# Expert 0's low weight parts move from GpSimd to VectorE, and the combine-weight products move behind the first step's second half

## What is computed

```
logits = einsum(x, gate_w); weights, indices = top_k(softmax(logits), 2), normalised
for i in 0..7:
    h   = silu(x @ w1[i]) * (x @ w3[i])        # 256 -> 1024
    out = out + (h @ w2[i]) * w_of_expert_i     # 1024 -> 256
```

## Time and profile before

| | us |
|---|---|
| median of 3 runs | 495.22 |
| the three runs | 494.84, 495.22, 1086.1 |
| span of the profiled execution (first to last instruction) | 492.8 |
| what lies around the span, by the median | 2.4 |
| own time of the profiled execution | not given beside its span |
| TensorE busy | 422.1 (86% of the span) |
| VectorE busy | 263.6 (53%) |
| ScalarE busy | 192.5 (39%) |
| GpSimd busy | 169.9 (34%) |
| mean granted TensorE clock | 0.926 |

### The profile page before, as it was taken

How to read it: one execution, slowest core, us unless ns; L and a number is a source line. 1 busy time by engine, 2 the same in 40 slices (tenths; PEclk the granted TensorE clock), 3 DMA queues, 4 the chain that set the end, 5 groups by cost and what they waited for, 6 DMA issues and landing times.

```text
span 492.8 us, 10407 instructions
## 1 busy us (share of the span) xinstructions
PE 422.1 (86%) x2557; PEld 365.9 (74%) x2558; DVE 263.6 (53%) x670; ACT 192.5 (39%) x334; POOL 169.9 (34%) x133
## 2 busy tenths in 40 slices
PE   0678984314999999999999999999999999999980
PEld 0556864313888889888888988888898888889870
DVE  7877869997454255433563564355356433653230
ACT  3446443301444246233542643354264334542230
POOL 5455434442023333322242333224233322532321
PEclk9979795555999999999999999999999999999995
DMA  6856885604415421541118118111811211121120
GB/s 196 297 179 206 272 268 157 200 1 139 161 23 160 149 32 32 203 105 23 30 21 287 32 21 283 32 26 21 287 32 21 32 30 23 21 32 32 21 32 11
DMA packets 33076, 50.92 MB, mean 103 GB/s; under 512 B 3335, under 2 KB 25095, under 8 KB 33063
## 3 DMA queue, kind: packets, MB, share of 16 engines
q1 hardware_dynamic: 24983, 38.44, 23.4%
q0 software_dynamic: 8080, 12.33, 12.8%
HBM read 39.36 MB, written 11.40 MB: 103 GB/s over the span
## 4 chain that ended last, share of the span: by engine, by line
PE 73%; DVE 7%; issue 2%; DMA 1%; POOL 1%; ACT 1%; ACTq 0%; POOLq 0%; DVEq 0%
PE bank L1312 64%; PE bank L1335 7%; PE bank L1319 2%; DVE ctx_sb L901 2%; DVE onehot_lo L986 1%; DVE rank L889 1%; DMA dg<-depool_rows,plugi 1%; PE bank L1266 1%; POOL dg L441 1%; DMA xblk<-z_rows,gidx 1%; PE bank L1191 0%; DVE batch L990 0%; POOL out L485 0%; DVE st L823 0%; DVE x_all L820 0%
## 5 line engine op out<-in xcount | busy, mean ns | idle before, releaser
L1312 PE MATMUL bank<-split,xT_hi 128*128 x592 | 166.8, 403 | 1.3 <-DVE xT_lo L1087 1.3
L1096 DVE TENSOR_TENSOR hmul<-gact,bank 128x512 f32<-128x512 f32 x74 | 50.9, 688 | 149.1 <-ACT gact L614 149.1
L485 POOL DMA_INDIRECT out<-yblk,itok x37 | 78.4, 2118 | 149.8 <-ACT yblk L621 138.2
L1312 PEld LDWEIGHTS bank<-split,xT_hi 128*128 128x128 f32 x592 | 106.9, 190 | 22.6 <-issue 1.9
L1312 PE MATMUL bank<-split,hT 128*128 (+1 forms) x888 | 115.4, 286 | 1.4 <-issue 0.8
L1312 PEld LDWEIGHTS bank<-split,hT 128*128 128x128 f32 x888 | 108.5, 191 | 2.1 <-issue 1.2
L614 ACT ACTIVATE gact<-bank 128x512 f32<-128x512 f32 x74 | 44.2, 598 | 158.9 <-PE bank L1312 158.8
L1312 PE MATMUL bank<-split,xT_lo 128*128 x296 | 93.7, 398 | 0.0
L477 POOL DMA_INDIRECT xblk<-z_rows,gidx x40 | 40.1, 1001 | 106.0 <-DVE gidx L1109 100.3
L321 DVE TENSOR_TENSOR split<-raw,split x21 | 48.1, 2293 | 37.6 <-ACT split L315 37.6
L1312 PEld LDWEIGHTS bank<-split,xT_lo 128*128 128x128 f32 x296 | 56.0, 189 | 13.5
(11 more groups left out here) (182 smaller groups left out, 332.4 us busy)
## 6 DMA issues: line engine op xcount, KB each, us to landing
raw<-in_L_ffn_w SPq DMA_DIRECT2D x24, 1024.0 KB, 8.0
ctx_sb<-in_ctx SPq DMA_DIRECT2D x4, 1024.0 KB, 6.4
x_all<-in_x SPq DMA_DIRECT2D x4, 512.0 KB, 8.3
depool_rows<-gact SPq DMA_DIRECT2D x4, 512.0 KB, 3.0
out<-x_all SPq DMA_DIRECT2D x4, 512.0 KB, 5.5
z_rows<-z SPq DMA_DIRECT2D x4, 512.0 KB, 3.9
xblk<-z_rows,gidx POOLq DMA_INDIRECT x40, 2.8
out<-yblk,itok POOLq DMA_INDIRECT x37, 4.7
```

What stands on the lines that cost most here:

```text
L485: pool.indirect_dma_start(out[:, :], bass.IndirectOffsetOnAxis(ap=itok[:, q:q + 1], axis=0), yblk[:, q, :], None, compute_op=ALU.add).then ...
L1096: dve.tensor_tensor(hmul[:, cols], gact[:, cols], p_lin[part][:, :], ALU.mult)\
L1312: mm = pe.matmul(out_, xp, w_, start=start and n == 0, stop=stop and n == 2)
```

## The change

GpSimd no longer makes low parts. VectorE makes those of w1 and w3 in two halves by columns, the first half of both ahead of `xT(0, 0)` and the second half ahead of `weight_rows`, and that of w2 at the end of step 0. TensorE waits for `lo_first` 1 and 2 ahead of the two halves of `up` in step 0; for step 1 it waits, as before, for `lo_ready`, which now rises at the end of VectorE's step 0. The list products of the combine weights stand behind `up(0, 1)` instead of behind `up(0, 0)`.

```
--- before.py
+++ after.py
@@ -458,17 +458,12 @@
                     pow2(k - 2)
 
 
-            split_lo(pool, 0, 0, 0, "lo_first")
-            split_lo(pool, 0, 0, 1, "lo_first")
-
-
             pool.wait_ge(s["hi_step"], 1)
             pool.wait_ge(s["bf16_ready"], 14)
             half = slice(0, B * TPB)
             pool.tensor_tensor(hi_idx[:, half, 1, :], hi_eq[:, half, :],
                                tiles_b[:, half].unsqueeze(2).broadcast_to([P, B * TPB, TABLE]), ALU.mult)\
                 .then_inc(s["tile_step"], 1)
-            split_lo(pool, 0, 0, 2, "lo_first")
 
             def block_rows(i, q):
 
@@ -1115,6 +1110,14 @@
                 dve.tensor_copy(wtok[:, q:q + 1], w_all[:, ds(i, 1)])
                 dve.tensor_copy(itok[:, q:q + 1], idx_all[:, ds(i, 1)]).then_inc(s["meta_ready"], 1)
 
+            def first_up(part):
+
+                cols = slice(part * HALF, (part + 1) * HALF)
+                dve.wait_ge(s["hi_ready"], 2)
+                dve.tensor_tensor(up_lo[:, 0, :, :, cols], raw_up[:, 0, :, :, cols],
+                                  up_hi[:, 0, :, :, cols].bitcast(f32), ALU.subtract)\
+                   .then_inc(s["lo_first"], 1)
+
             def step(i, q, half, word):
                 later = not isinstance(i, int) or i > 0
                 h(i, 0)
@@ -1127,6 +1130,10 @@
                     weights_out()
                 h(i, 1)
                 hT(i, q, 0)
+                if not later:
+                    split_lo(dve, 0, 0, 2, "lo_first")
+                    dve.wait_ge(s["lo_first"], 3)
+                    dve.sem_inc(s["lo_ready"], 3)
 
                 with dve.If(word & F_CHUNK):
                     e = expert(word)
@@ -1141,10 +1148,10 @@
             dve.wait_ge(s["x1_rows"], 16 * B)
             for b in range(B):
                 dve.wait_ge(z_out[b], 16)
-            dve.wait_ge(s["lo_first"], 3)
-            dve.sem_inc(s["lo_ready"], 3)
+            first_up(0)
             xT(0, 0)
             next_index(2, 0, 1)
+            first_up(1)
             weight_rows(0)
             weight_rows(1)
             def drain(i, q):
@@ -1354,16 +1361,21 @@
                 later = not isinstance(i, int) or i > 0
                 slot = word & 1
                 pe.wait_ge(s["xTlo_ready"], i + 1)
-                pe.wait_ge(s["lo_ready"], expert(word) * 3 + 2)
+                if later:
+                    pe.wait_ge(s["lo_ready"], expert(word) * 3 + 2)
+                else:
+                    pe.wait_ge(s["lo_first"], 1)
 
                 up(slot, q, 0)
-                if not later:
-                    lists(p_w, hi_w, (8, 11))
                 if later:
                     hT(i - 1, 1)
                 xT(i + 1, 1 - q, half + q)
 
+                if not later:
+                    pe.wait_ge(s["lo_first"], 2)
                 up(slot, q, 1)
+                if not later:
+                    lists(p_w, hi_w, (8, 11))
                 hT(i, 0)
                 if later:
                     down(i - 1, 1 - q, expert_before(word), (word >> PREV_BIT) & 1)
```

## The result

488.61 us median (488.37 to 489.01, 4 runs) beside 494.84 for the kernel before (493.31, 494.84 and 495.22): a ratio of 0.9888, 95% interval 0.9869 to 0.9907, so it is some 1.1% faster, which is clear of the noise. One further run of the kernel before took 1086.1 us and is left out. The forecast was 491.7 with 488.2 to 495.0, so the time lies in the range, at its lower end. It lies outside the narrower 490.3 to 493.3 that the prediction gave the forecast itself, and 0.3 us from what rival (a) gave. The profiled execution took 488.38 us with a span of 486.7; the one of before has 492.8, a difference of 6.1 us, and what follows accounts for that.

What follows compares the result with a forecast made beforehand. The prediction took the time as when the blocks start plus TensorE's work in the steps; -10.5 + 0.4 + 4.3 - 0.5 + 2.4 + 0.4 = -3.5 us on 495.2 gave 491.7 us, range 488.2 to 495.0.

Steps and rivals of the forecast that it cites:

- rival (a): TensorE's clock holds through the 4.3 us wait and step 0 gets it as before: -6.3, 488.9 us; chance 0.18.
- The gain, -10.5: Router, ahead of the table: three VectorE stalls beside GpSimd's low parts leave, 2.3 + 3.9 + 4.3 = 10.5 us earlier.
- the first stall: VectorE's cast of 8 elements beside GpSimd's first low part: 4.1 us raw, of which 2.3 us come through.
- rival (b): The first stall isn't GpSimd's doing, or something else holds the last batch: -1.2, 494.0 us; chance 0.10.
- Rival (d): TensorE at half clock holds the router's chain, so only the third stall comes through: +2.7, 497.9 us; chance 0.02.
- The first half ahead of step 0, +0.4: VectorE's 2.29 us low part ahead of `xT_lo` exceeds its idle 2.05 us: `up(0, 0)` starts 0.4 us later.
- The wait of step 1, +4.3: Ahead of `up(1, 0)` TensorE stands idle 4.3 us for the low part of w2; bounds 3.8 and 4.8.
- Given back, -0.5: Step 1's own wait for VectorE, 0.44 us visible at 136.29, goes: -0.5 us (0.2 to 1.0).
- The clock, +2.4 and +0.4: TensorE's clock falls after step 1's wait, +2.4 us (0 to 3.4); step 0 must also earn it, +0.4 (0 to 1.2).
- (c): The clock stays low well beyond step 1; through two whole steps it costs 9.5, 498.8 us; chance 0.04.

Runs made afterwards that it cites:

- experiment 5: The changed kernel plus an unread GpSimd instruction, the low part of w1 at its old place: 491.41 us.
- experiment 7: The changed kernel plus an unread GpSimd instruction, the low part of w3 at its old place: 492.41 us.
- experiment 9: The changed kernel plus an unread GpSimd instruction, the low part of w2 at its old place behind GpSimd's list product: 492.97 us.
- experiment 6: The changed kernel plus half of w1's low part (1024 of 2048 columns) on GpSimd at its old place, unread: 489.20 us.
- experiment 2: The changed kernel with the low part of w2 made in VectorE's idle time ahead of `weights_out`, not at the end of step 0: 483.43 us.
- experiment 3: The changed kernel with `lo_ready` raised in two parts, so step 1 starts without w2's low part and only the down product waits for it: 485.04 us.
- experiment 1: The changed kernel with 34 unused transposes of the identity filling TensorE's wait at the end of step 0: 486.38 us.
- the seven executions: The profiled executions with the wait at the end of step 0: one each of the changed kernel, experiment 4, experiment 5, experiment 6, experiment 7, experiment 8 and experiment 9.
- experiment 11: The kernel of experiment 2 with 16, 5 and 5 unused transposes in TensorE's waits between the index lists and step 0: 483.33 us.
- experiment 4: The changed kernel with the combine-weight list products back behind the first half of `up` in step 0: 489.04 us.
- experiment 8: The changed kernel plus a GpSimd memset of 2048 float32 a partition behind its list product, where w2's low part was: 490.08 us.
- experiment 12: The kernel of experiment 2 with the unused transposes of experiment 11 and GpSimd's last list product made by VectorE: 482.83 us.

## Why the prediction was right, term by term

**The gain, -10.5.** Measured 10.8 (10.9 less 0.15), and experiments 5, 7 and 9 give its parts: 2.6, 3.9, 4.3 for 2.3, 3.9, 4.3. The reason for the first number, that TensorE's logits cover the first two us of the first stall, is shown by experiment 6: half an instruction holds VectorE for 2.0 us longer and costs 0.4 in the trace, and the transposes start only 0.1 us later. What the sum left out is that they run 0.3 us shorter behind the logits. The rival (b), that the one-input cast isn't held by GpSimd, fell with experiment 5. Rival (d) fell with the table at 105.12.

**The first half ahead of step 0, +0.4.** Measured +0.1. `xT_lo` started 0.3 us later against the table than before, about as the sum had it, but TensorE's 0.43 us between `xT_lo` and its first matmul became 0.23, so most of the delay was taken up. Why that interval is shorter wasn't tried.

**The wait of step 1, +4.3.** Measured +4.03, and its cause, the low part of w2 at the end of VectorE's queue, is shown by experiments 2 and 3, which each take the gap ahead of step 1 away. Neither `up(0, 1)` nor the list products waited for VectorE, as forecast.

**Given back, -0.5.** Step 1 gave back 1.0 us where the clock is kept (experiment 1, 12.64 us for 13.60), and the same in the changed kernel (0.58 lost in all, of which the clock took 1.56). I had counted little more than the visible 0.44 us at 136.29 and named 1.0 as the bound. The rest is what a break costs the matmuls beside it: before, `down(0)` and the next `up` took 3.23 and 3.06 us behind the break and now 5.67 in one run, 0.6 less, and the transposes ahead of it 0.44 for 0.61; the 0.26 that `up(1, 0)` is longer behind the new wait goes off again.

**The clock, +2.4 and +0.4.** It fell, as forecast, and the cost was 1.5 to 1.6 us, shown by experiment 1: with 0.8 us the most mis-sized term. I took the low time from the two long stretches of the trace of before, 5.6 and 4.2 us of work (the share in the earlier trace rows gives 34.61 for the end of the first, not 34.56); here the clock was low for 3.4 us (from the shares 0.71 and 0.88 in the stretches above). The +0.4 for step 0 didn't appear in the profiled execution, 4.96 us for 4.97; with 4.4 to 5.5 us in the seven executions it is less a cost of the change than a spread of the kernel. So is part of the +2.4: experiment 9, with 6.8 us at half, has 5.48 us for `up(1, 0)`, 2.4 over the 3.06 at full clock. The Trainium skill (TensorE: Matmul & The Clock Gate, "HAM oscillation") describes a long wait between groups of matmuls that makes the next group start slow. Experiment 1 agrees, with 3.06 us for 4.62 once the wait is filled, and experiment 11 shows the same at the start of step 0, 2.9 for 4.96.

So rival (a) has the measured time within 0.3 us by luck. Its second half, that step 0 gets the clock as before, came true, but its reason is wrong: the clock doesn't hold, and the terms that came out better than forecast make up for the 1.6 us. The forecast has the right mechanism in every term but the last +0.4, and a sum that is too high; the time alone would have chosen (a), and only the trace and experiment 1 decide. Each of the six terms came out on the faster side, by 0.3 to 0.8 us, 2.6 together. With the 0.15 us ahead of the cast they make the 2.7 us between the sum of -3.5 and the -6.2 of the trace; the other 0.4 of the 3.1 us between 491.7 and 488.6 is that the sum stood on 495.2 and the median of the kernel before is now 494.8. That the time lies in the stated range is owed to the room that the range left for rival (a). The rival on the slower side, (c), needed the clock to stay low for 11.8 us of work; it stayed low for 3.4, and for 6.8 at most in the seven executions. That it falls wasn't an accident of one execution: it fell in all seven.

## What to carry to other kernels

A GpSimd instruction can cost its whole length on VectorE's side: look for VectorE instructions that are much longer than their twins, and put GpSimd's timeline beside them; then ask what is late next, because here 4.1 us of holding cost 2.6, and 2.0 cost 0.4. When work moves to another engine, the place in that engine's queue decides more than its length: the same 2.29 us cost some 5 us more at the end of the step than in the idle time ahead of `weights_out`. A counter that stands for several things makes a reader wait for the last of them. A sum whose terms all have the right reason can still be off to one side; here each cost was taken a little too high.

## What the runs showed of the hardware that I had not expected

A GpSimd memset, which reads nothing, held a VectorE instruction with one input, and the held instruction (L985) waited for two GpSimd instructions in a row, 3.28 us for 0.40. In experiment 9, with a subtraction in the memset's place, it waited for one.

In the changed kernel the clock fell with the first matmul behind a wait of 4.06 us (full at 122 to 122.5, half by 123). That moment is a matter of the single execution: behind or in waits of 3.96 to 4.39 us at the same place it fell 0.8, 0.6 and 0.4 us before the next matmul in experiments 9, 4 and 6, and 0.2, 0.8 and 1.1 us after it in 7, 8 and 5. In experiment 11 it fell some 1.2 us after work had begun again behind a wait of 2.26 us; in experiment 12, with a wait of 2.10 us, it didn't fall, nor in experiment 1 behind 0.29 us. One execution of each is recorded, so that the wait of 2.26 us was the cause isn't shown.

The same 12 matmuls at the full clock take 2.80 us in a dense run and 3.06 behind a break, and the transposes of the router 1.81 and 2.09 us at half clock: small idle times cost something beside their own length.
